# Centring and gate as four 64x64 corners, and the variance of two layers from whole float32 squares, in a four-layer triangle kernel

## What is computed

```python
for l in range(4):
    v = group_norm(x)                       # 32 groups of 2 channels, over all positions
    xn = layer_norm(v) * w + b              # over the 64 channels; layer 3 has none
    left  = mask * sigmoid(xn @ Wlg) * (xn @ Wl)
    right = mask * sigmoid(xn @ Wrg) * (xn @ Wr)
    gate  = sigmoid(xn @ Wg)
    t = einsum('ikd,jkd->ijd', left, right) # layers 0, 1; 'kjd,kid->ijd' in layers 2, 3
    x = x + (layer_norm(t) @ Wo) * gate     # gate before or after Wo, by the layer
```

## Time and profile before

| | us |
|---|---|
| median of the runs (lowest, highest) | 1425.36 (1421.46, 1428.51) |
| profiled execution, its own time | 1427.8 |
| profiled execution, span | 1425.6 |
| PE busy / PEld busy | 1231.4 (86%) / 686.5 (48%) |
| DVE busy | 983.5 (69%) |
| ACT busy | 920.8 (65%) |
| POOL busy | 525.5 (37%) |

### The profile page before, as it was taken

One profiled execution on the slowest core, in us unless ns is written; L12 is line 12 of the kernel. 1 busy time (PEld: TensorE's weight loads), 2 busy tenths in 40 slices (PEclk: granted clock), 3 DMA queues, 4 the chain that ended last, 5 costly groups with the idle time before them and its releaser, 6 DMA issues. The chain is left out here.

```text
span 1425.6 us, 39778 instructions
## 1 busy us (share of the span) xinstructions
PE 1231.4 (86%) x11486; PEld 686.5 (48%) x11486; DVE 983.5 (69%) x2692; ACT 920.8 (65%) x1849; POOL 525.5 (37%) x490
## 2 busy tenths in 40 slices
PE   0799998789799998999982999999888788899897
PEld 0455555434344544674331555567544344467443
DVE  6577776368779999226991888842299899931587
ACT  0577775399677777227992888842499677722676
POOL 0355553045355655003551666620155200000365
PEclk9999999999889999999995999999999999999999
DMA  8011111578623332797758555549799544469898
GB/s 296 23 51 50 50 50 64 140 230 263 202 90 105 105 110 84 211 297 217 204 158 326 156 170 176 185 142 298 251 288 282 183 156 155 149 186 313 263 315 267
DMA packets 222432, 258.73 MB, mean 181 GB/s; under 512 B 54177, under 2 KB 209057, under 8 KB 222369
## 3 DMA queue, kind: packets, MB, share of 16 engines
q1 hardware_dynamic: 193920, 232.75, 52.1%
q10 hardware_dynamic: 28448, 25.17, 5.4%
HBM read 139.89 MB, written 117.96 MB: 181 GB/s over the span
## 5 line engine op out<-in xcount | busy, mean ns | idle before, releaser
L1036 DVE SCALAR_TENSOR_TENSOR lr<-ps,mask,act_out 128x128 f32 (+5 forms) x1152 | 278.8, 310 | 51.1 <-ACT act_out L785 42.9
L1195 POOL TENSOR_TENSOR rstd<-ve,half_col 128x6 f32<-128x6 f32 x144 | 190.4, 1323 | 232.0 <-DVE ve L1003 196.5
L1240 POOL TENSOR_TENSOR new_ring<-val,lr 128x384 f32<-128x384 f32 x96 | 104.0, 1084 | 372.1 <-issue 297.8
L569 PE MATMUL ps<-w_parts,val 64*128 64x256 bf16 (+1 forms) x1728 | 199.7, 310 | 18.4 <-DVE lr L1036 17.7
L785 ACT ACTIVATE act_out<-ps 128x384 f32<-128x384 f32 x384 | 176.1, 483 | 50.5 <-PE ps L579 34.3
L1228 POOL TENSOR_TENSOR val<-act_out,gate_ring 128x384 f32<-128x384 f32 x96 | 99.8, 1040 | 224.8 <-ACT act_out L855 189.5
L679 PE MATMUL ps<-in_ring,k 128*128 128x384 f32 x288 | 124.4, 517 | 26.2 <-DMA in_ring<-t_scratch 23.0
L838 ACT ACTIVATE sq<-ps 128x384 f32<-128x384 f32 x192 | 105.7, 551 | 54.0 <-PE ps L679 52.0
L1087 DVE COPY cen<-ps 128x384 f32<-128x384 f32 x48 | 26.8, 558 | 159.1 <-PE ps L637 159.1
L637 PE MATMUL ps<-lr 64*128 64x192 f32 (+3 forms) x896 | 125.8, 331 | 9.8 <-DVE lr L1036 5.2
L761 ACT ACTIVATE cen<-ps,gn 128x384 f32<-128x384 f32 x144 | 83.8, 582 | 77.1 <-PE ps L524 73.8
(11 more groups left out here) (108 smaller groups left out, 2290.0 us busy)
## 6 DMA issues: line engine op xcount, KB each, us to landing
gate_scratch<-gate_ring SPq DMA_DIRECT2D x192, 192.0 KB, 2.2
gate_ring<-gate_scratch SPq DMA_DIRECT2D x96, 384.0 KB, 3.9
lr<-x_scratch SPq DMA_DIRECT2D x72, 384.0 KB, 4.9
in_ring<-t_scratch SPq DMA_DIRECT2D x72, 384.0 KB, 3.9
x_scratch<-new_ring SPq DMA_DIRECT2D x48, 384.0 KB, 3.4
in_ring<-x_scratch SPq DMA_DIRECT2D x96, 192.0 KB, 2.4
lr<-x SPq DMA_DIRECT2D x6, 1536.0 KB, 15.5
t_scratch<-cen SPq DMA_DIRECT2D x96, 96.0 KB, 4.0
```

The costliest lines, as they stand in the source:

```text
L569: mm = nc.tensor.matmul(banks[h][:, :, 0:P], moving(x, s)[half(h), N * r:N * r + P], proj_weights(w, h)[:, 0:2 * P], start=start, stop=sto ...
L1036: ins = nc.vector.scalar_tensor_tensor(out5[:, h, lo // 2:hi // 2, :, m], ps[:, 4 + 2 * r + h, lo:hi].rearrange("p (a e) -> p a e", e=2), ...
L1195: nc.gpsimd.tensor_tensor(rstd[:, s % 2, :], ve[:, s % 2, :], half_col[:, :], ALU.pow)\
```

## The change

**Corners.** `centre` and `gate` of the layers with a norm become four 64x64 matmuls of 192 columns each (`corners`): one for each half q of the partitions (array rows) and each image row e (array columns). The result lies with the image row on the partitions and the half in the bank: banks 0 and 1 hold the centred tile in columns 0 to 191 and the gate in columns 192 to 383. The gate turns the layout back, so what is stored is as before. cen, sq, xn and the projection's input are in the turned layout; `glu` writes for (half r, row g) where it wrote for (half h, row r).

**Order and waits.** The centred tile has one buffer where it had two. `centre(n+4)` moves between the two projections of tile n and waits for `cen(n+3)` and for the sigmoid of `gate(n)`; `gate(n)` waits for `cen(n+3)`; ScalarE puts the copy `centred(n+4)` between its two sigmoids and the square, now read from cen, behind them. The variance moves to bank 3, one buffer, and waits for `var_eps` of the tile before.

**Whole squares.** In layers 1 and 2 `variance` is three float32 matmuls with the squares themselves as stationary matrix; `square_low` is gone there.

**Loop.** TensorE's 48 steps of stage A in these layers are written out straight, without the hardware loop.

```diff
--- before.py
+++ after.py
+WHOLE_VAR = (False, True, True, False)
...
-                def centre(n, i, s):
+                def corners(first, weights, x, start, stop):
+
+                    for q in range(2):
+                        for e in range(2):
+                            mm = nc.tensor.matmul(ps[C * e:C * e + C, q, first:first + N], weights[half(q), half(q)],
+                                                  x[half(q), N * e:N * e + N], start=start, stop=stop,
+                                                  skip_group_check=True)
+                    return mm
+
+                def centre(n, i, s, gated):
...
-                    slot_free(pe, a_sq, base + n - 1)
-                    slot_free(pe, a_ve, base + n - 1)
-                    nc.tensor.matmul(ps[:, s % 2, 0:TILE], w_centre[:, :], in_ring[:, s, :] if l else x_all[:, n, :],
-                                     start=True, stop=True).then_inc(a_z, 1)
+                    slot_free(pe, a_cen, base + n)
+                    if gated:
+                        pe.wait_ge(a_gate, base + n - RING + 1)
+                    corners(0, w_centre, in_ring[:, s, :] if l else x_all[:, n, :], True, True).then_inc(a_z, 1)
...
-                    pe.wait_ge(a_sq_lo, base + n + 1)
+                    slot_free(pe, a_ve, base + n)
+                    if WHOLE_VAR[l]:
+                        pe.wait_ge(a_sq, base + n + 1)
+                        for j in range(CHUNKS):
+                            mm = nc.tensor.matmul(ps[:, 3, 2 * j:2 * j + 2], sq[:, s % 2, P * j:P * j + P], k_sel,
+                                                  start=True, stop=True)
+                        mm.then_inc(a_var, 1)
+                        return
...
-                def gate(n, s):
+                def gate(n, s, centred):
...
+                    if ln:
+                        if centred:
+                            pe.wait_ge(a_cen, base + n + RING)
+                        for w, x in passes:
+                            mm = corners(N, gate_weights(w), moving(x, s), (w, x) == passes[0], (w, x) == passes[-1])
+                        mm.then_inc(a_gate_mm, 1)
+                        return
                     slot_free(pe, a_gate, base + n)
...
                 def step(n, i, s, ahead):
-                    gate(n, s)
+                    gate(n, s, ahead >= 3)
                     if ln and ahead >= 1:
                         spread(n + 1, (s + 1) % RING)
                     project(n, s, 0)
+                    if ln and ahead >= 4:
+                        centre(n + 4, i + 1, s, True)
                     project(n, s, 1)
-                    if ln and ahead >= 4:
-                        centre(n + 4, i + 1, s)
                     if ln and ahead >= 3:
                         variance(n + 3, (s + 3) % RING)
...
-                over_tiles(pe, step)
+                if ln:
+                    for n in range(TILES):
+                        step(n, n // RING, n % RING, TILES - 1 - n)
+                else:
+                    over_tiles(pe, step)
...
+                    nc.scalar.activation(cen[:, s, :].rearrange("p (h j) -> p h j", h=2), ps[:, 0:2, 0:N], ACT.Identity,
+                                         bias=gn_cb).then_inc(a_cen, 1)
+
+                def squared(n, s):
+                    act.wait_ge(a_cen, base + n + 1)
                     slot_free(act, a_var, base + n - 1)
-                    nc.scalar.activation(cen[:, s, :], ps[:, s % 2, 0:TILE], ACT.Identity, bias=gn_cb)\
-                        .then_inc(a_cen, 1)
-                    nc.scalar.activation(sq[:, s % 2, :], ps[:, s % 2, 0:TILE], ACT.Square, bias=gn_cb)\
-                        .then_inc(a_sq, 1)
+                    nc.scalar.activation(sq[:, s % 2, :], cen[:, s, :], ACT.Square).then_inc(a_sq, 1)
...
-                    nc.scalar.activation(gate_ring[:, s, :], ps[:, 3, 0:TILE], ACT.Sigmoid, bias=gate_bias[:, 0:1])\
-                        .then_inc(a_gate, 1)
+                    slot = gate_ring[:, s, :].rearrange("p (r j) -> p r j", r=ROWS)
+                    nc.scalar.activation(slot if ln else gate_ring[:, s, :], ps[:, 0:2, N:2 * N] if ln else ps[:, 3, 0:TILE],
+                                         ACT.Sigmoid, bias=gate_bias[:, 0:1]).then_inc(a_gate, 1)
...
                     sigmoids(n, s, 0)
+                    if ln and ahead >= 4:
+                        centred(n + 4, s)
                     sigmoids(n, s, 1)
                     if ln and ahead >= 4:
-                        centred(n + 4, s)
+                        squared(n + 4, s)
...
-                    nc.vector.tensor_scalar(ve[:, s % 2, :], ps[:, s % 2, TILE:TILE + 2 * CHUNKS], LN_EPS, None,
+                    nc.vector.tensor_scalar(ve[:, s % 2, :], ps[:, 3, 0:2 * CHUNKS], LN_EPS, None,
...
-                        for h in range(2):
+                        for g in range(2):
+                            h, row = (r, ROWS * n + g) if ln else (g, m)
...
-                    if ln and ahead >= 3:
+                    if halved and ahead >= 3:
                         square_low(n + 3, (s + 3) % RING)
```

More of the change, by code:

```diff
@@ L58 @@
 LATE = 14
+WHOLE_VAR = (False, True, True, False)
+LOWS = tuple(sum(1 for m in range(l) if not WHOLE_VAR[m]) for l in range(LAYERS))
 T_SCALE = (1.0, 1.0, 1.0 / N, 1.0)
@@ L521, in centre @@
                         pe.wait_ge(in_loaded[s], in_count(l) + 16 * (i + 1))
[L522 to L525 removed]
+                    slot_free(pe, a_cen, base + n)
+                    if gated:
+                        pe.wait_ge(a_gate, base + n - RING + 1)
+                    corners(0, w_centre, in_ring[:, s, :] if l else x_all[:, n, :], True, True).then_inc(a_z, 1)
                 def variance(n, s):
[L529 removed]
+                    slot_free(pe, a_ve, base + n)
[6 more added lines that the diff above has]
+                        return
+                    pe.wait_ge(a_sq_lo, LOWS[l] * TILES + n + 1)
                     for j in range(CHUNKS):
                         for part in (sq_high, sq_low):
[L532 removed]
+                            mm = nc.tensor.matmul(ps[:, 3, 2 * j:2 * j + 2],
                                                   part[:, s % 2, P * j:P * j + P], sel_bf[:, :],
@@ L604, in phase_a @@
                 if ln:
-                    centre(0, 0, 0)
-                    centre(1, 0, 1)
+                    centre(0, 0, 0, False)
+                    centre(1, 0, 1, False)
                     variance(0, 0)
                     variance(1, 1)
-                    centre(2, 0, 2)
-                    centre(3, 0, 3)
+                    centre(2, 0, 2, False)
+                    centre(3, 0, 3, False)
                     spread(0, 0)
                     variance(2, 2)
-                over_tiles(pe, step)
+                if ln:
[3 more added lines that the diff above has]
+                    over_tiles(pe, step)
             def keep_clock(bank, count):
@@ L807, in phase_a @@
                 if ln:
[L808 to L811, removed]
+                    for n in range(RING):
+                        centred(n, n)
+                        squared(n, n)
                     high(0, 0)
@@ L989, in phase_a @@
                 ln = HAS_LN[l]
+                halved = ln and not WHOLE_VAR[l]
                 out5 = lr_view(l).rearrange("p a e (h r) -> p h a e r", h=2)
@@ L1032, in glu @@
                     if HAS_MASK[l]:
-                        for h in range(2):
+                        for g in range(2):
+                            h, row = (r, ROWS * n + g) if ln else (g, m)
                             for t, (lo, hi) in enumerate(((0, P), (P, COLS))):
                                 ins = nc.vector.scalar_tensor_tensor(
[L1037 to L1040, removed]
+                                    out5[:, h, lo // 2:hi // 2, :, row],
+                                    ps[:, 4 + 2 * r + g, lo:hi].rearrange("p (a e) -> p a e", e=2),
+                                    mask4[:, t, h, bass.ds(row, 1)],
+                                    sig[:, g, lo:hi].rearrange("p (a e) -> p a e", e=2), ALU.mult, ALU.mult)
                         ins.then_inc(a_free, 1)
@@ L1043, in glu @@
                         nc.vector.tensor_tensor(
-                            out5[:, :, :, :, m],
-                            ps[:, 4 + 2 * r:6 + 2 * r, 0:COLS].rearrange("p h (a e) -> p h a e", e=2),
-                            sig.rearrange("p h (a e) -> p h a e", e=2), ALU.mult).then_inc(a_free, 1)
+                            out5[:, r, :, :, bass.ds(ROWS * n, ROWS)].rearrange("p a e g -> p g a e"),
+                            ps[:, 4 + 2 * r:6 + 2 * r, 0:COLS].rearrange("p g (a e) -> p g a e", e=2),
+                            sig.rearrange("p g (a e) -> p g a e", e=2), ALU.mult).then_inc(a_free, 1)
                 def step(n, i, s, ahead):
@@ L1059, in step @@
                     glu(n, 0)
-                if ln:
+                if halved:
```

(1 more changed line is left out.)

## The result

The changed kernel took 1448.8 us (median of four runs, 1446.3 to 1457.7) against 1424.1 (the table of before has the higher of its two middle runs, 1425.4): a ratio of 1.018, 95% interval 1.013 to 1.023. The prediction was 1424.5 with a range of 1411 to 1438. It was wrong: slower, and outside the range.

A forecast was written before the change was run, and what follows sets the result against it. Bounds taken: TensorE in layer 0, VectorE in layer 1, TensorE fullest in layer 2. 3.4 + 0 - 6.4 + 2.1 = -0.9 on the profiled 1427.8, itself 2.4 above the median: 1424.5 us, range 1411 to 1438.

The forecast's parts named there:

- Layer 2, -6.4 us: Layer 2, stage A: TensorE's period of 3.24 against 3.39 a tile, -6.4 us, bounds -11 to 0.
- The loop: Layer 0, stage A: TensorE's loop turn goes, but the ring through `a_free` binds first.
- Layer 0, +3.4: Layer 0, stage A: centring enters the `a_free` ring, 4.03 against 3.95 a tile, +3.4 us, bounds +2 to +9.
- Layer 1, 0: Layer 1, stage A: VectorE's ring keeps its 3.63, so nothing changes; bounds 0 to +6 us.
- Openings, +2.1: Start of each layer: single-buffered centring waits for ScalarE's copy, +0.7 a layer, +2.1 us, bounds 0 to +4.
- 1 (TensorE collects): Layer 0: TensorE stays the bound, period 3.38, -24.5 instead of +3.4, so 1397 us; chance 0.13.
- the ring: Layer 0, `a_free`: first wide projection, second sigmoid, glu, back to TensorE; 3.70 before, 4.03 with the centring.
- 2: Layer 2's gain at its bound and free openings: 1417 us; chance 0.08.
- 3 (ScalarE's order): Layers 0 and 1: copy delays the second sigmoid and glu; at 0.15 beyond, +6.5 in each, 1437.5 us; chance 0.17.
- 4: Corner matmuls do not overlap: centring 0.65, gate as before, layers 0 and 2 slower, near 1463 us; chance 0.05.
- 5: Each change of array shape delays the next product everywhere, 0.18 more in layers 0 and 1, 1440 us; chance 0.02.

The follow-up runs named there:

- Experiment 2: Kernel before with TensorE's 48 stage A steps of layers 0 to 2 written straight: 1438.3 us, ratio 1.0091; with the store ahead of the gather too, 0.9987.
- experiments 4 and 5: Changed kernel, store ahead of gather, plus: layer 0's centring ahead of first projection (1.0008) or behind second (0.9999); or bfloat16 halves in layers 1 and 2 (1.0011).
- `keep` first: Changed kernel, SyncE's layer 2 steps straight, store of the next pair ahead of the gather: 1436.8 us, 1.0079 against the kernel before; run again, 1.0051.
- Its repeat: The changed kernel run once more, unedited, on the same chip: ratio 1.0156 against the kernel before.

## Why the prediction was wrong, step by step

- **Layer 2, -6.4 us: the step that failed.** Its terms for TensorE were right (3.26 for 3.24; variance to gate 844.17 - 843.41 = 0.76, which is 0.67 and the 0.09 for the change of shape; low parts of 0.56). The sentence that failed is "SyncE's loads wait for a_z, which now comes about 0.8 us earlier in the tile". The gathers waited for the landing of a store, in a ring of 6.65 us a pair. I had checked that the loads were released in time, not how fast they could come at all. In their place the runs showed a ring that cannot feed 3.26 a tile, turns of 7.0 to 8.7 us where packets met it, and a stage 12.1 us longer. With that ring taken away, layer 2 gained 4.3 us of the 6.4.
- **The loop, priced at its turns alone.** I wrote that TensorE's loop turn goes, and looked for its price on TensorE. Straight steps raise the instruction packets from 36 to 92 (to 76 in the kernel before), and these cost on another engine's transfers. The row was on the page of before (`q8 instruction: 36`), and I gave it no term. Experiment 2 puts 12 us on this in the kernel before.
- **Layer 0, +3.4: right mechanism, size off.** 8.1 came, inside the bounds of 2 to 9. The centring added its 0.33. Mis-sized were two handoffs, each by some 0.08: sigmoid to glu 0.25 where I took 0.18, and glu to TensorE 0.15 where I took 0.06 from layer 1. There the wait stands in the third pass; here it stands at the first product of the tile. The text named 0.15 as the upper end and did not take it.
- **Layer 1, 0: right.** 3.63 in three tiles of four, the fourth 3.95 for 3.87, 3.69 to 3.71 in the mean, TensorE waiting 0.20 for glu, the stage 0.1 us shorter.
- **Openings, +2.1: half of it came.** From the first centring to the first gate: in layer 1 403.89 - 392.82 = 11.07 us, before 397.04 - 386.85 = 10.19, +0.9; but in layer 0 11.08 against 10.88, +0.2, and in layer 2 11.16 against 11.19. In all +1.1, inside the 0 to +4.
- **Rivals.** 1 (TensorE collects) was barred by the ring, as said. 2 did not come either: with SyncE's ring out of the way layer 2 runs at 3.26, not at 3.14. 3 (ScalarE's order) was not the cause, but it is near: it showed in experiments 4 and 5 once other waits had gone. Against 4 stands the centring's own time, 202.26 - 201.93 = 0.33 and not 0.65; against 5, layer 1's stage, which did not get longer. The rival that came true, SyncE's ring with late landings, was not on the list; the range fell with it.

## What to carry to other kernels

When an engine gets faster, list every ring that feeds it, the DMA queue's own among them, and compute each ring's shortest turn: issues, plus landing, plus what stands between them in that queue's program. A ring at 3.33 under a demand of 3.39 looks harmless and is the next bound. And a transfer that waits for all DMA engines is as late as the latest of them, so anything that runs on one alone, code being fetched for instance, belongs in the sum wherever a ring has no slack. Before moving an operation into a gap, look at what it waits for in that place, not only at the gap.

## What was not expected of the hardware

- **Fetching code disturbs data.** 16 KB packets of instructions, one every 7 us, held one DMA engine for 0.9 to 1.8 us each; stores beside them landed after up to 5.1 us instead of 2.6, and one DMA issue took up to 1.7 us instead of 0.6. TensorE did not wait for its code: with `keep` first it was busy 120.00 of 120.00 us while 20 packets came. The Trainium skill (Runtime: NRT & Kernel Launch, Instruction fetch mechanics) has the program streamed in blocks of 16 KiB over a DMA queue of the sequencer's own, and calls the cost mostly hidden. For the engine that runs the code the traces agree; for the kernel they don't, with 12 us in experiment 2.
- **A short wait can cost more in clock than in time.** 2.24 us of idle time were followed by 6.8 us at half clock, and the stall cost 5.4 us in all. Its repeat had 2.37 us of waiting and then 10 us at half clock; the three waits of experiment 2, of 2.3, 2.1 and 1.7 us, were followed by 3.4, 3.4 and none.
- **A gather released by a landing is no proof of a bound.** In before each of the 17 gathers from 812 us on started 0.15 to 0.21 us behind a landing, and taking that wait away changed nothing (1.0011).
